# Expert stage: plain f32 products, wide token rows, and output rows scattered from the tile loop

## What is computed

```
gp = jax.nn.softmax(xt @ w_group + b_group, axis=-1)
...
combine = jax.nn.one_hot(flat_e, E, dtype=xt.dtype) * (g_prob * e_prob)[:, None]
h = jax.nn.relu(jnp.einsum('td,edf->etf', xt, w1) + b1[:, None, :])
y = jnp.einsum('etf,efd->etd', h, w2) + b2[:, None, :]
out = jnp.einsum('te,etd->td', combine, y)
...
x = _layernorm(x + moe_out, ln2_g, ln2_b)      # end of the block
...
x = _layernorm(x + _L0_ffn_ref(x, ...), axis=-1)   # end of the layer: x is the block's input
```

## Time and profile before

| | us |
|---|---|
| median of 3 runs | 969.0 |
| lowest and highest | 966.13, 969.98 |
| profiled execution, its whole time | 972.12 |
| its span, first to last instruction | 970.4 |
| gate stage | 0 to about 82 |
| attention stage | about 82 to 766 |
| expert stage | 766 to 970.4 |

### The profile page before, as it was taken

The page is one execution under the profiler, slowest core; times in us unless marked ns, Lnnn a source line. Parts: engine busy times, 40 slices in busy tenths (PEclk is TensorE's granted clock), DMA queues, the critical chain, the costliest instruction groups (busy, mean ns, idle before and its releaser), DMA issues. The chain is left out here.

```text
span 970.4 us, 12521 instructions
## 1 busy us (share of the span) xinstructions
PE 694.6 (72%) x4120; PEld 453.2 (47%) x4121; DVE 513.7 (53%) x1231; ACT 263.2 (27%) x382; POOL 166.9 (17%) x172
## 2 busy tenths in 40 slices
PE   5844488878887889887798977888787633999400
PEld 4733254545554454544455544545454312888300
DVE  3884245564562645536364562645645492555286
ACT  2201141423423223143231423413133350222002
POOL 3003410112201121020111202101010053000063
PEclk9975677988898797979768997978897655999855
DMA  6464312213112040312204041111220372222322
GB/s 222 140 209 170 91 35 66 55 57 76 46 48 75 23 109 3 76 50 73 66 2 109 19 92 45 46 33 32 47 78 13 110 249 81 66 65 59 120 68 100
DMA packets 64109, 75.73 MB, mean 78 GB/s; under 512 B 7665, under 2 KB 54197, under 8 KB 63673
## 3 DMA queue, kind: packets, MB, share of 16 engines
q1 hardware_dynamic: 57770, 62.62, 23.2%
q0 software_dynamic: 1680, 7.21, 2.2%
q10 hardware_dynamic: 4608, 5.24, 1.5%
HBM read 32.84 MB, written 16.52 MB: 51 GB/s over the span
## 5 line engine op out<-in xcount | busy, mean ns | idle before, releaser
L1335 DVE TENSOR_REDUCE a_nmax<-wide 128x4 f32<-128x1024 f32 x128 | 153.2, 1217 | 79.6 <-PE wide L973 79.2
L1185 ACT ACTIVATE a_E<-wide 128x1024 f32<-128x1024 f32 x128 | 123.3, 1013 | 48.9 <-PE wide L973 48.9
L855 POOL TENSOR_TENSOR a_rstd<-a_var,nhalf 128x2 f32<-128x2 f32 x40 | 27.9, 698 | 545.2 <-DVE a_var L1300 545.2
L133 PE MATMUL bank<-a_th,dw 128*128 128x256 f32 x320 | 107.0, 481 | 6.4 <-DVE a_x L1310 5.0
L973 PE MATMUL wide<-a_Q,a_K 50*128 50x256 f32 x512 | 72.3, 373 | 33.8 <-DMA a_Q<-a_mrow 19.2
L973 PE MATMUL wide<-a_K,a_Q 48*128 48x256 f32 x512 | 72.6, 372 | 24.7 <-DMA a_Q<-a_stage 17.6
L962 PE MATMUL bank<-a_E,a_va 128*32 128x256 f32 x1024 | 89.3, 479 | 0.3 <-DVE a_cu L1357 0.3
L133 PE MATMUL bank<-dw,a_th 128*128 128x256 f32 x320 | 87.9, 408 | 0.0
L133 PEld LDWEIGHTS bank<-a_th,dw 128*128 128x128 f32 x320 | 70.0, 236 | 33.5 <-issue 14.7
L1164 ACT ACTIVATE a_th<-bank 128x512 f32<-128x512 f32 x48 | 28.6, 596 | 197.7 <-PE bank L920 197.7
L973 PEld LDWEIGHTS wide<-a_Q,a_K 50*128 50x128 f32 x512 | 45.3, 221 | 74.1 <-ACT a_E L1185 32.3
(11 more groups left out here) (262 smaller groups left out, 1131.0 us busy)
## 6 DMA issues: line engine op xcount, KB each, us to landing
a_K<-a_stage SPq DMA_DIRECT2D x96, 128.0 KB, 3.1
a_Q<-a_stage SPq DMA_DIRECT2D x96, 128.0 KB, 3.3
w<-in_w_dram SPq DMA_DIRECT2D x1, 4096.0 KB
x_d<-a_x SPq DMA_DIRECT2D x16, 256.0 KB, 2.4
m_w<-in_w_dram SPq DMA_DIRECT2D x1, 4096.0 KB, 21.8
xs_d<-g_zeros POOLq DMA_DIRECT2D x1, 2944.0 KB, 10.1
m_xs<-xs_d SPq DMA_DIRECT2D x23, 128.0 KB, 2.3
ys_d<-m_yb ACTq DMA_DIRECT2D x23, 128.0 KB, 2.5
```

The costliest lines, as they stand in the source:

```text
L133: last = pe.matmul(out, left[c], right[c], start=(start and c == 0), stop=(stop and c == n - 1))
L855: pool.tensor_tensor(rstd[l][:, :], var[l][:, :], nhalf[:, 0:T], ALU.pow).then_inc(rs_ok[l].s, 1)
L1185: act.activation(Ex[g % 2][:, kt, :, :], pW[r % 2][:, :].rearrange("p (h s) -> p h s", h=4), ACT.Exp, scale=HD ** -0.5).then_inc(ex.s, 1)
L1335: dve.tensor_reduce(nmax[l][:, t, :].rearrange("p (h c q e) -> p h q c e", h=HALVES, c=C, q=2)[:, jj // 2, jj % 2, :, :], pW[r % 2][:, :]. ...
```

## The change

It touches the expert stage and the fill of `xs_d`.

- **Rows.** A row of `xs_d` has 514 numbers instead of 256: x5, x4, the gate and the token's number (`xr` in SBUF). Padding rows carry the number 2048, which is out of range. The fill writes such a blank row to every place, from one row per partition.
- **Products.** The weights are no longer split. `plain` multiplies f32 by f32. The biases enter by one fast product each: `sel` picks for each tile its expert's row of `bs`, which holds b1 and b2 as rounded part and rest (16 rows). DVE's subtractions and bias adds go; ACT copies the transposes and applies ReLU before the second transpose.
- **Normalisations.** They run tile by tile in the loop, on the rows in sorted order, since row, gate, x5 and x4 lie together in `xs`: DVE `first_b` to `first_e` for tile c, `second_a` to `second_d` for c-1, `shift` for c-2; POOL two powers; ACT the last step into `o`.
- **Output.** POOL scatters `o` to the output by the token numbers `ids`, dropping padding. `ys_d` and the gather go.
- **Loop.** The steps are written out, without the hardware loop; `xs` has six buffers; only TensorE still reads the expert from `texp_i`. SP loads x5 and x4 in 16 transfers before w2.

```diff
-            pool.memset(zeros[:, :], 0.0).then_inc(zero_ok, 1)
-            pool.wait_ge(zero_ok, 1)
-            pool.dma_start(xs_d.rearrange("(p n) d -> p (n d)", p=P), zeros[:, :]).then_inc(zero_out, 16)
+            pool.memset(blank[:, 0:2 * D + 1], 0.0).then_inc(zero_ok, 1)
+            pool.memset(blank[:, 2 * D + 1:ROW].bitcast(I32), B * S).then_inc(zero_ok, 1)
+            pool.wait_ge(zero_ok, 2)
+            pool.dma_start(xs_d.rearrange("(p n) d -> p n d", p=P),
+                           blank[:, :].unsqueeze(1).to_broadcast([P, TILES, ROW])).then_inc(zero_out, 16)
...
+            for b in range(B):
+                sp.dma_start(xr[:, b * T:(b + 1) * T, 0:D], x5_d[b].rearrange("p (t d) -> p t d", t=T)).then_inc(x5_in, 16)
+            for b in range(B):
+                sp.dma_start(xr[:, b * T:(b + 1) * T, D:2 * D], x4_d[b].rearrange("p (t d) -> p t d", t=T)
+                             ).then_inc(x4_in, 16)
             sp.dma_start(w2[:, :, :, :], I["w2"].rearrange("e (c p) f -> p e c f", p=P)).then_inc(w_in, 16)
+            sp.wait_ge(b_lo, 1)
+            sp.dma_start(bs[E:2 * E, :].bitcast(F32), bl[:, :].bitcast(F32)).then_inc(bl_in, 16)
             sp.wait_ge(xs_w, 16 * NT)
...
+            for c in range(TILES):
+
+                done(sp, u_ok, c - XB)
+                sp.dma_start(xs[c % XB][:, :], xs_d[c * P:(c + 1) * P, :]).then_inc(xs_in[c % XB], 16)
+                if c == XB - 1:
+                    sp.dma_start(ids[:, :, :], xs_d.rearrange("(t p) d -> p t d", p=P)[:, :, GATE:TOKEN + 1].bitcast(I32)
+                                 ).then_inc(ids_in, 16)
...
+            pool.wait_ge(b_hi, 1)
+            pool.tensor_tensor(bl[:, :], bias[:, :], bs[0:E, :].bitcast(F32), SU).then_inc(b_lo, 1)
+            pool.wait_ge(x5_in, 16 * B)
+            pool.wait_ge(x4_in, 16 * B)
+            pool.wait_ge(id_ok, 2)
             pool.wait_ge(slot_ok, 1)
             for n in range(NT):
                 pool.indirect_dma_start(out=xs_d, out_offset=bass.IndirectOffsetOnAxis(ap=slot[:, n:n + 1], axis=0),
-                                        in_=x5[:, n, :], in_offset=None).then_inc(xs_w, 16)
+                                        in_=xr[:, n, :], in_offset=None).then_inc(xs_w, 16)
...
+            for c in range(TILES + 4):
+                if there(c):
+                    done(pool, var1_ok, c)
+                    pool.tensor_tensor(rstd1[c % 2][:, :], var1[c % 2][:, :], nhalf[:, 0:1], ALU.pow).then_inc(rs1_ok, 1)
+                if there(c - 1):
+                    done(pool, var2_ok, c - 1)
+                    done(pool, o_ok, c - 1 - UB)
+                    pool.tensor_tensor(rstd2[(c - 1) % UB][:, :], var2[(c - 1) % UB][:, :], nhalf[:, 0:1], ALU.pow
+                                       ).then_inc(rs2_ok, 1)
+                if there(c - 3):
+                    if c == 3:
+                        pool.wait_ge(ids_in, 16)
+                    done(pool, o_ok, c - 3)
+                    pool.indirect_dma_start(out=flat_out, out_offset=bass.IndirectOffsetOnAxis(
+                                                ap=ids[:, c - 3, 1:2], axis=0),
+                                            in_=o[(c - 3) % 2][:, :], in_offset=None, bounds_check=B * S - 1,
+                                            oob_is_err=False).then_inc(out_w[(c - 3) % 2], 16)
...
+            act.wait_ge(b_in, 32)
+            act.activation(bs[0:E, :], bias[:, :], ACT.Copy).then_inc(b_hi, 1)
             act.wait_ge(g_in, 1)
             act.activation(gx[:, :, :], gl[:, :, :], ACT.Exp).then_inc(g_ex, 1)
...
+                if there(c - 3):
+                    k = c - 3
+                    done(act, mr_ok, k)
+                    if k >= 2:
+                        act.wait_ge(out_w[k % 2], 16 * (k // 2))
+                    act.activation(o[k % 2][:, :], u[k % UB][:, :], ACT.Identity, scale=rstd2[k % UB][:, 0:1],
+                                   bias=mr[k % UB][:, 0:1]).then_inc(o_ok, 1)
...
+            dve.tensor_scalar(sel[:, :, :], texp[0:2 * E, :].unsqueeze(2).to_broadcast([2 * E, TILES, P]),
+                              which[2][:, 0:1], None, ALU.is_equal).then_inc(sel_ok, 1)
...
+            def second_a(c):
+                done(dve, rs1_ok, c)
+                done(dve, c_ok, c)
+                done(dve, o_ok, c - UB)
+                dve.scalar_tensor_tensor(u[c % UB][:, :], z[c % 2][:, :], rstd1[c % 2][:, 0:1], xs[c % XB][:, D:2 * D],
+                                         MM, AD).then_inc(u_ok, 1)
```

434 lines of the change are left out of this document (160 added, 274 removed).

## The result

| | before | after |
|---|---|---|
| median of four executions, us | 969.5 | 957.1 |
| lowest and highest | 966.1, 970.0 | 955.0, 957.8 |
| profiled execution, whole time | 972.1 | 957.8 |
| its span | 970.4 | 955.9 |

A forecast was written before the change was run, and what follows sets the result against it. TensorE was taken to bound the expert loop, with a 59.1 us end leaving it idle. -45.3 + 19.5 - 4.5 + 1 = -29.3 took 972.1 to 942.8 profiled, 939.7 as median; range 928 to 956.

The forecast's parts named there:

- The end, -45.3: Last product to program end: 13.8 us instead of 59.1, between 11 and 17, as only the last tile's chain is left.
- The head, -4.5: Expert stage before the first row transpose: transpose at 811 instead of 815.5 us, between -8 and +4.
- late exponential: Head: ACT's bias conversion moves the exponential from 767.03 to about 769.7; dropping TensorE's bias products nearly cancels that.
- The loop, +19.5: First transpose to last product: 4.75 us a tile against 3.90, 18.7 over 22 tiles, plus slow start, less 1 at drain.
- the biases move from DVE to two fast products: Loop, each tile: the bias products cost 0.25 and 0.12 us, in a new period of 4.75.
- bound on the period, 5.1: Loop: sign that the sum is wrong at that step if a tile's period is above 5.1 us.
- The start of the loop: First tiles: partly at clock 0.50, as before, where plain products cost 1.5 to 2 us more; +1.8 in all.
- The first stage, +1: Fill of xs_d grows to 6.1 MB, landing in 20 us beside loads fetched a product ahead; between -1 and +4.
- Row loads: Rival, loop: loads of rows into six buffers set the pace, period 5.5 us, 952 in all; chance 0.14.
- The scatters were short: Rival, head: scatters stay long because three streams share the DMA engines, 7.7 us later, 947; chance 0.12.
- The handovers did not bind: Rival, loop: handshake delays among DVE, POOL and ACT add up to a 5.5 us period, 956; chance 0.07.
- The clock was 1.00 in the loop: Rival, loop: TensorE's clock drops, 956 at 0.84, 972 and up at 1.2 GHz for seven tiles; chance 0.06.

The follow-up runs named there:

- e7: Changed kernel with a memset, three two-operand subtractions and three constant additions of unused work on DVE beside the 16 scatters; 961.1 us.
- e4: Changed kernel with the fill of xs_d issued only after TensorE's seventh transpose batch in the first stage; 954.8 us, ratio 0.985 to the kernel before.

## Why the prediction was wrong, step by step

- **The end, -45.3: right** (-45.1). Issue of the last scatter 8.8 us after the last product where 9.8 was summed, from there to the end 5.2 instead of 4.0: two misses of about 1 us cancel.
- **The head, -4.5: right in sum** (-5.0), partly by luck. It is made of a faster run of scatters (19.1 us from the first start to the last, where 811.11 - 784.43 = 26.7 were and 15 x 1.26 + 1.4 = 20.3 were forecast), against a late exponential: 3.4 us after the stage's start. That it nearly cancels with the products that had made DVE wait was too hopeful: the first scatter starts 19.6 us after the stage's start, where 18.3 were before. And from the last scatter to the first transpose 5.7 us pass, where 4.4 did and 5.3 were forecast. POOL's subtraction of the biases beside DVE's L1678 (1.24 us instead of 0.22) was not in the sum. The selector table's 1.4 us were not needed, and they covered for the other two. The first transpose comes 44.4 us after the stage's start, where 44.9 was the forecast.
- **The loop, +19.5: wrong, +30.9. This is the term that failed.** The step that failed is the one by which the biases move from DVE to two fast products, at 0.25 and 0.12 us. It took the columns for the whole price. The products over 16 rows cost 1.12 us a tile, of which 0.77 is the change of height, four times a tile. The steps beside it were sized well (layers 1.72 and 1.72 for 1.71 and 1.73) or 0.28 too high, which hid part of the miss: 4.38 + 0.37 = 4.75 was forecast, 4.10 + 0.35 + 0.77 = 5.22 came, and 4.45 would have come without the change of height. The prediction's own bound on the period, 5.1, points to the place. Over 22 tiles the longer period is 10.3 us too much. From the first product to the last only 7.8 of that show, because the drain gave back 2.5 more than forecast: its two steps without a first layer take 3.20.
- **The start of the loop was too low: +5.4 instead of +1.8.** I priced plain products at clock 0.50 for as long as the clock had stayed down before. That was 5.6 us, and it stayed down for 10.8, which costs some 1.6 us more and is in part chance (+2.7 and +3.6 in `e7` and `e4`). The rest is longer work, the changes of height among it.
- **The first stage, +1: wrong, +4.2.** The step is "it lies beside loads that are fetched a product ahead". A load fetched one product ahead was no cover for a fill that fills the DMA engines for 28 us: TensorE's wait for x grew from 0.88 to 3.85 us at the third batch. That is just over the upper bound of 4.
- **The rivals.** Row loads of 257 KB landed in 2.7 us and TensorE never waited for one in the loop. The scatters were short. The handovers did not bind: DVE idles 2.9 us a tile waiting for TensorE, so its tile takes 2.3 us and not 3.2. The clock was 1.00 in the loop. None of the four came true: the time is outside the range for a reason that was not on the list.

The experiments were not needed to see this price: the trace of the kernel before has it, in a stage that the prediction read only for the pace of plain products. In the attention stage a fast product of 4 rows and 512 columns adds a bias, between products of 128 rows, at clock 1.00 (710 to 718 us):

```profile
712.39 1.99 PE L133 MATMUL bank<-a_th,dw 128*128 128x256 f32 x8
714.31 0.18 PEld L935 LDWEIGHTS bank<-a_chunk_r,a_bsplit 4*128 4x128 f32 x1 [0.33 <-issue]
714.31 0.49 PE L935 MATMUL bank<-a_chunk_r,a_bsplit 4*128 4x512 f32 x1
714.73 1.59 PEld L133 LDWEIGHTS bank<-a_th,dw 128*128 128x128 f32 x8 [0.24 <-issue]
714.73 1.99 PE L133 MATMUL bank<-a_th,dw 128*128 128x256 f32 x8
716.56 1.89 PE L133 MATMUL bank<-dw,a_th 128*128 128x256 f32 x8
```

It is the same picture: each load starts with its product though PEld was idle. The bias product takes 714.73 - 714.31 = 0.42 us, twice its columns' 0.21, and the eight records around it 1.92 and 1.83 where the earlier trace rows give 1.73. By these rows two such products between 128-row products cost about 0.4 us each above their columns, 0.8 a tile; 0.77 came. The head's one-row bias products show nothing of it: they are four in a row at 1.2 GHz.

## What to carry to other kernels

Give the small products in a stream of full ones the full height: pad the contraction to 128 rows with zeros, or put all the small ones side by side, or move them to an idle engine. A product's price is its columns only when its weights can be loaded beside the product ahead, and the PEld rows show that: look whether a load starts with its product though PEld was idle, in any stage of a trace that you already have. And before a transfer is called hidden, look at what else the DMA engines carry while it runs, and at who waits for that; moving it may only move the bill.
